# Decoder layer on one core: head 0's first projection in the gate chain, and the delta-rule loop begun at body 1

## What is computed

```python
mixed = hidden_states @ W_qkv                       # 512 -> 8*128 (q) + 8*128 (k) + 16*128 (v)
mixed = _causal_conv_silu(mixed.transpose(0, 2, 1), conv_w).transpose(0, 2, 1)   # 4 taps
z = (hidden_states @ W_z).reshape(Bb, Tt, HV, DV)
beta = sigmoid(hidden_states @ W_b)
g = -jnp.exp(A_log) * softplus(hidden_states @ W_a + dt_bias)
q = _l2norm(q) * DK ** (-0.5);  k = _l2norm(k)      # each key head serves two value heads
def step(S, inp):                                   # over 256 tokens
    S = S * exp(gt)
    v_adj = (vt - einsum('bhk,bhkv->bhv', kt, S)) * bt
    S = S + kt * v_adj
    o = einsum('bhk,bhkv->bhv', qt, S)
o = o * rsqrt(mean(o * o) + EPS) * norm_weight * silu(z)
return o.reshape(Bb, Tt, VALUE_DIM) @ W_out
```

## Time and profile before

| | us |
|---|---|
| median of three runs | 2235.8 |
| profiled execution | 2231.07 |
| its span, first to last instruction | 2229.3 |
| `prepare`, to its last instruction | 0 to 64.95 |
| clearing block and what lies around it | 64.95 to 70.61 |
| opening of the main block | 70.61 to 81.3 |
| body 0, body 1 | 81.3 to 124.9, to 166.1 |
| body 32 begins | about 1414.7 |
| mean granted clock of the span | 0.962 |

### The profile page before, as it was taken

The page is one execution under the profiler, slowest core; times in us unless marked ns, Lnnn a source line. Parts: engine busy times, 40 slices in busy tenths (PEclk is TensorE's granted clock), DMA queues, the critical chain, the costliest instruction groups (busy, mean ns, idle before and its releaser), DMA issues. The chain is left out here.

```text
span 2229.3 us, 55828 instructions
## 1 busy us (share of the span) xinstructions
PE 2042.1 (92%) x19672; PEld 1482.0 (66%) x19672; DVE 1724.6 (77%) x4017; ACT 1524.6 (68%) x4326; POOL 708.7 (32%) x610
## 2 busy tenths in 40 slices
PE   5699999999999999999999999858999999857998
PEld 3477777777777777777777777646666666534544
DVE  7677877877877877877877877645788888856997
ACT  3588888888888887887888887635656666633443
POOL 6312112112112112112112112113676777741332
PEclk8799999999999999999999999779999999978999
DMA  3100100100100100100100000053333333231111
GB/s 78 53 10 14 43 10 15 42 10 19 38 10 19 38 10 19 38 10 19 38 10 20 23 10 19 11 179 107 96 106 105 102 99 96 62 123 48 60 59 43
DMA packets 119728, 106.33 MB, mean 48 GB/s; under 512 B 11984, under 2 KB 93904, under 8 KB 119632
## 3 DMA queue, kind: packets, MB, share of 16 engines
q1 hardware_dynamic: 119632, 105.29, 15.0%
HBM read 70.66 MB, written 34.60 MB: 47 GB/s over the span
## 5 line engine op out<-in xcount | busy, mean ns | idle before, releaser
L589 PE MATMUL proj<-xn_hi,w_lo 128*128 x768 | 362.4, 472 | 0.0
L590 PE MATMUL proj<-xn_lo,w_hi 128*128 x768 | 303.8, 396 | 0.0
L591 PE MATMUL proj<-xn_hi,w_hi 128*128 x768 | 303.0, 394 | 0.0
L976 DVE SCALAR_TENSOR_TENSOR qkv<-conv_in,taps,qkv 128x512 f32<-128x512 f32 x384 | 278.2, 745 | 0.0
L1202 POOL TENSOR_TENSOR o_scale<-o_var,neg_half 128x4 f32<-128x4 f32 x68 | 67.6, 1010 | 549.1 <-DVE o_var L997 549.0
L1218 POOL TENSOR_TENSOR k_len<-sumsq,pos_half 128x4 f32<-128x4 f32 x32 | 46.9, 1466 | 571.6 <-DVE sumsq L1151 571.6
L1095 DVE TENSOR_TENSOR i_less_r<-bank_c,join_mask 128x256 f16<-128x256 f32 x330 | 124.3, 417 | 101.9 <-PE bank_c L653 101.3
L895 ACT ACTIVATE inv<-bank_b 128x256 f16<-128x256 f32 x330 | 111.3, 382 | 96.1 <-PE bank_b L674 92.5
L591 PEld LDWEIGHTS proj<-xn_hi,w_hi 128*128 128x128 f32 x768 | 144.2, 188 | 34.4
L589 PEld LDWEIGHTS proj<-xn_hi,w_lo 128*128 128x128 f32 x768 | 144.3, 188 | 24.0
L1699 ACT ACTIVATE probs_t<-ps_s 128x512 f32<-128x512 f32 x128 | 69.6, 596 | 130.4 <-PE ps_s L1547 130.3
(11 more groups left out here) (288 smaller groups left out, 5799.2 us busy)
## 6 DMA issues: line engine op xcount, KB each, us to landing
out_t<-o_out SPq DMA_DIRECT2D x68, 256.0 KB, 2.0
o_raw<-out_t SPq DMA_DIRECT2D x32, 512.0 KB, 5.4
w_raw<-in_L_attn_W_qkv_dram SPq DMA_DIRECT2D x32, 256.0 KB, 2.8
wq_dram<-wq_q SPq DMA_DIRECT2D x48, 128.0 KB, 2.0
x_sb<-in_x_dram SPq DMA_DIRECT2D x16, 256.0 KB, 2.7
w_raw<-in_L_attn_W_z_dram SPq DMA_DIRECT2D x16, 256.0 KB, 2.7
x_in<-in_x_dram SPq DMA_DIRECT2D x16, 256.0 KB, 5.6
wq_raw<-in_L_ffn_w_gate_dram SPq DMA_DIRECT2D x16, 256.0 KB, 2.7
```

The costliest lines, as they stand in the source:

```text
L589: pe.matmul(out, w_lo[:, k, cols], sh.xn_hi[:, k, tok], start=(k == 0), stop=False)
L590: pe.matmul(out, w_hi[:, k, cols], sh.xn_lo[:, k, tok], start=False, stop=False)
L591: product = pe.matmul(out, w_hi[:, k, cols], sh.xn_hi[:, k, tok], start=False, stop=(k == KT - 1))
L976: dve.scalar_tensor_tensor(out=out, in0=conv_in[:, j, :, k:k + T], scalar=taps[:, j, k:k + 1], in1=out, op0=ALU.mult, op1=ALU.add).then_in ...
```

## The change

The nine tiles that a projection uses move to `prepare`'s allocations, as `sh.*`. `prepare` makes pair 0's whole projection of head 0 with them. `delta_rule` starts at n = 1: its block `zero` gives every semaphore the count that body 0 would have left; the mask, the decay sums, the gates, the tanh of z and the key lengths for body 1 stand ahead of the loops. TensorE gets a loop of its own for pairs 1 to 3 of head 0.

```diff
@@ prepare, sync: behind the small loads
+                for j in range(TILES):
+                    load_tile(j)
@@ prepare, gpsimd: first
+                pool.memset(sh.conv_in[:, :, :, 0:TAPS - 1], 0.0).then_inc(pad_done, 1)
@@ prepare, vector
                 dve.tensor_scalar(sh.norm_half[:, :], norm_raw[:, :], 0.5, None, ALU.mult)
+                split(0)
+                split(1)
+                dve.wait_ge(taps_done, 1)
...
+                dve.tensor_copy(sh.taps[:, 0:2, :], by_kind[:, :, 0, :])
+                dve.tensor_copy(sh.taps[:, 2:4, :], sh.conv_half[:, 2 * HK:2 * HK + 2, :]).then_inc(taps_done, 1)
+                dve.wait_ge(taps_done, 2)
+                split(2)
                 dve.wait_ge(consts_done, 2)
...
                 dve.reciprocal(um1[:, :, :], um1[:, :, :]).then_inc(gate_dve, 1)
+                split(3)
...
                 dve.tensor_scalar(g[:, :, :], g[:, :, :], -1.0, -MAX_DECAY, ALU.mult, ALU.max).then_inc(gate_dve, 1)
+                split(4)
+                convolve(0)
                 dve.wait_ge(gate_dve, 13)
...
                 dve.tensor_tensor(g_lo[:, :, :], g[:, :, :], g_hi[:, :, :].bitcast(F32), ALU.subtract).then_inc(gate_dve, 1)
+                split(5)
+                convolve(1)
                 dve.wait_ge(gate_act, 7)
...
+                for j in range(2):
+                    silu(j)
+                for j in range(2, 4):
+                    convolve(j)
+                dve.wait_ge(ss_ps, 1)
+                dve.tensor_scalar(sh.sumsq[:, :], ps_t[0][:, 0:8], EPS, None, ALU.add)
@@ prepare, tensor: behind the transposes of the gates
+                def project(j):
+                    pe.wait_ge(w_lo_done, j + 1)
+                    if j < 2:
+                        pe.wait_ge(xt_done, 2 * R)
+                        pe.wait_ge(lo_done, 4 + BEFORE)
+                        pe.wait_ge(hi_done, 4)
+                    else:
+                        pe.wait_ge(proj_ev, j - 1)
...
+                for j in range(3):
+                    project(j)
                 pe.wait_ge(consts_done, 2)
                 pe.wait_ge(gate_dve, 13)
...
+                for j in range(3, TILES):
+                    project(j)
+                pe.wait_ge(sq_done, 1)
+                pe.wait_ge(proj_ev, TILES - 1)
+                for c in range(8):
+                    last = pe.matmul(ps_t[0][:, c:c + 1], ...)
+                last.then_inc(ss_ps, 1)
@@ prepare, scalar
                 for i in (R - 2, R - 1):
                     copy_gates(i, i % 2)
+                    split(i - R + 2)
+                split(2)
...
                 act.activation(ln_u[:, :, :], u[:, :, :], ACT.Ln).then_inc(gate_act, 1)
+                split(3)
+                for j in range(2):
+                    tile_copy(j)
+                    split(4 + j)
+                tile_copy(2)
                 act.wait_ge(cum_ps, 1)
...
+                tile_copy(3)
+                act.wait_ge(conv, 2 * (TAPS - 1))
+                act.activation(sh.th[:, :, :], sh.qkv[:, 0:2, :], ACT.Tanh).then_inc(th_done, 1)
+                tile_copy(4)
+                act.wait_ge(silu_done, 2)
+                act.activation(sh.th[:, :, :], sh.qkv[:, 0:2, :], ACT.Square).then_inc(sq_done, 1)
+                tile_copy(5)
@@ delta_rule, block zero
-                    sp.dma_start(w_raw[j][:, :, :], ...)
...
+            for done in once:
+                act.sem_inc(done, 1)
...
-                pool.memset(qkv[:, :, :], 0.0)
                 pool.memset(z_silu[:, :, :], 0.0)
-                pool.memset(k_len[:, :], 1.0)
                 pool.memset(pos_half[:, :], 0.5)
-                for s in S:
-                    pool.memset(o[s][:, :, :], 0.0)
-                    pool.memset(inv_r[s][:, :, :].bitcast(F32), 0.0)
+                pool.memset(o[0][:, :, :], 0.0)
+                pool.memset(inv_r[0][:, :, :].bitcast(F32), 0.0)
+                for done in twice:
+                    pool.sem_inc(done, 2)
...
-                dve.memset(conv_in[:, :, :, :], 0.0)
-                for z in (z_raw, z_th):
-                    dve.memset(z[:, :, :], 0.0)
-                dve.memset(gate[:, :, :], 0.0)
-                dve.memset(gate_off[:, :, :], 0.0)
+                dve.memset(o[1][:, :, :], 0.0)
+                dve.memset(inv_r[1][:, :, :].bitcast(F32), 0.0)
...
-                dve.memset(g_cols[:, :, :], 0.0)
@@ delta_rule, tensor
-                    decay_sums(0, s, None)
-                with pe.Fori(0, HK) as g:
+                    decay_sums(1, s, 1)
+                with pe.Fori(1, PAIRS) as p:
+                    step(p, 0, p)
+                with pe.Fori(1, HK) as g:
@@ delta_rule, scalar
-                for j in range(LATE):
-                    split(0, j)
-                mask_gates(0, None)
+                mask_gates(1, 1)
+                act.activation(z_th[:, :, :], z_raw[:, :, :], ACT.Tanh, scale=0.5).then_inc(z_th_done, 1)
                 for g in range(HK):
-                    step(PAIRS * g, True, g, None)
+                    if g:
+                        step(PAIRS * g, True, g, None)
@@ delta_rule, vector: as on scalar, and ahead of it
-                for j in range(LATE):
-                    split(j, j + 1)
-                head_taps(0)
+                dve.tensor_copy(g_cols[:, :, :], sh.gates[:, 2:4, 8:16]).then_inc(cols_done, 1)
+                key_gate(1)
+                off_gate(1)
@@ delta_rule, gpsimd
+                pool.tensor_tensor(k_len[:, :], sumsq[:, 4:8], pos_half[:, :], ALU.pow).then_inc(len_done, 1)
+                with pool.Fori(1, STEPS) as n:
+                    step(n, True)
```

More of the change, by code:

```diff
@@ L23 @@
 W_COLS = 6 * P
+RAW_TILES = 3
 TAPS = 4
@@ L75, in prepare @@
     sh.gates = keep("gates", [P, 2 * (STEPS + 1), 16], F32)
+    sh.w_raw = [keep(f"w_raw{i}", [P, KT, P], F32) for i in range(RAW_TILES)]
+    sh.w_hi = keep("w_hi", [P, KT, W_COLS], F32R)
+    sh.w_lo = keep("w_lo", [P, KT, W_COLS], F32R)
+    sh.taps = keep("taps", [P, 4, TAPS], F32)
+    sh.conv_in = keep("conv_in", [P, 4, 2, T + TAPS - 1], F32)
+    sh.qkv = keep("qkv", [P, 4, 2 * T], F32)
+    sh.th = keep("th", [P, 2, 2 * T], F32)
+    sh.z_raw = keep("z_raw", [P, 2, 2 * T], F32)
+    sh.sumsq = keep("sumsq", [P, 8], F32)
     with ExitStack() as st:
@@ L242, in high_part, with split, convolve, silu @@
                                         xn_t[:, odd, k, :].rearrange("p (k t) -> p k t", k=KT)).then_inc(hi_done, 1)
+                def split(j):
+                    dve.wait_ge(w_hi_done, j + 1)
+                    cols = slice(P * j, P * j + P)
+                    dve.tensor_tensor(sh.w_lo[:, :, cols], sh.w_raw[j % RAW_TILES][:, :, :], sh.w_hi[:, :, cols].bitcast(F32),
+                                      ALU.subtract).then_inc(w_lo_done, 1)
+                def convolve(j):
+                    moved = sh.qkv[:, j, :].rearrange("p (b t) -> p b t", b=2)
+                    dve.wait_ge(proj_ev, j + 1)
+                    dve.wait_ge(pad_done, 1)
+                    for k in range(TAPS - 1):
+                        if k:
+                            dve.wait_ge(conv, (TAPS - 1) * j + k)
+                        dve.scalar_tensor_tensor(out=moved, in0=sh.conv_in[:, j, :, k:k + T], scalar=sh.taps[:, j, k:k + 1],
+                                                 in1=moved, op0=ALU.mult, op1=ALU.add).then_inc(conv, 1)
+                def silu(j):
+                    dve.wait_ge(th_done, 1)
+                    dve.scalar_tensor_tensor(out=sh.qkv[:, j, :], in0=sh.th[:, j, :], scalar=1.0, in1=sh.qkv[:, j, :],
+                                             op0=ALU.add, op1=ALU.mult).then_inc(silu_done, 1)
                 dve.memset(sh.gates[:, 0:2, :], 0.0)
@@ L340, in _ @@
                 last.then_inc(ba_turned, 1)
+                def project(j):
[6 more added lines that the diff above has]
+                        pe.wait_ge(proj_ev, j - 1)
+                    cols = slice(P * j, P * j + P)
+                    for k in range(KT):
+                        pe.matmul(ps_t[j % 2][:, :], sh.w_lo[:, k, cols], sh.xn_hi[:, k, 0:N2], start=(k == 0), stop=False)
+                        pe.matmul(ps_t[j % 2][:, :], sh.w_hi[:, k, cols], sh.xn_lo[:, k, 0:N2], start=False, stop=False)
+                        last = pe.matmul(ps_t[j % 2][:, :], sh.w_hi[:, k, cols], sh.xn_hi[:, k, 0:N2], start=False,
+                                         stop=(k == KT - 1))
+                    last.then_inc(proj_ps, 1)
+                for j in range(3):
+                    project(j)
                 pe.wait_ge(consts_done, 2)
@@ L499, in _ @@
             def _(pe):
-                pe.sem_inc(ss_ps, FIRST)
+                for done in (w_hi_done, w_lo_done, proj_ps, proj_ev):
+                    pe.sem_inc(done, TILES)
+                for s in S:
+                    for done in (r_ps, r_done, x_ps, x_done, t_done):
+                        pe.sem_inc(done[s], LEVELS)
```

(10 more changed lines are left out.)

98 lines of the change are left out of this document (57 added, 41 removed).

## The result

| | before | after |
|---|---|---|
| median of the runs timed together, us | 2236.67 (4 runs) | 2201.76 (4 runs, 2201.1 to 2202.54) |
| ratio, 95% interval | | 0.9847 [0.9835, 0.9859] |
| profiled execution, us | 2231.07 | 2202.18 |
| its span, us, and mean clock | 2229.3, 0.962 | 2200.5, 0.962 |
| first stage ends | 64.95 | 78.41 |

The account below looks back on a forecast made before the run. It took TensorE's filled delta-rule loop as the bound, with stretches ahead nearly empty of TensorE work and VectorE ending the gate chain. +13.4 - 1.7 - 4.6 - 41.7 = -34.6 us, from the 2235.8 median to 2201; range 2194 to 2210.

Parts of the forecast that it names:

- point 1: Main loop: one body goes and a new first body of 43.1 us replaces two taking 84.8; gain 41.7 us.
- point 2: Loop's opening: masks start after one small copy, other work hides behind them; 6.1 us instead of 10.69, gain 4.6.
- point 3: Clearing block: fewer clears but new semaphore increments at 48 ns; body from 4.6 to 2.9 us, gain 1.7.
- One sign of being wrong: Clearing block: the prediction called itself wrong if this block came out above 4.7 us.
- point 4: Gate chain: VectorE's 14.0 us of added work, less covered waits, plus collisions with GpSimd, lengthens it by 13.3 us.
- Rival C: Gate chain: GpSimd's block masks also collide with VectorE's low parts and tap copies, +3.0 us, 2204; chance 0.10.
- point 5: Gate chain on TensorE: tiles 3 to 5 start cold, squares end at 78.2, together with VectorE; +13.4 us.
- the last signature in the prediction: Gate chain's end: if TensorE's sums of squares stand clearly ahead of VectorE's last tap, VectorE alone sets the end.
- A: Clearing block and gate chain: semaphores nearly free, collisions fall into waits; -38.7 us, 2197; chance 0.15.
- B: Gate chain: TensorE stays at 1.2 GHz for all six tiles, +24 instead of +13.4, 2212; chance 0.10.
- D: Gate chain: tiles go in lockstep for raw buffers, 61 us later, so slower than before, 2249; chance 0.03.
- E: Main loop: TensorE's new loop copy makes its queue late at two first bodies, 2 to 4 us, 2205; chance 0.06.

Follow-up runs that it names:

- experiment 2: The changed kernel run again with no edit: 2200.52 us (4 runs), ratio 0.9837 to the kernel before.
- experiment 8: Changed kernel plus fourteen 512-column TensorE products that nothing reads, in the clearing block and around the decay sums: 2196.02 us.
- experiment 4: Changed kernel without GpSimd's block masks (clear and 14 selects) and without its join-mask products: 2196.24 us.
- experiment 3: Changed kernel with GpSimd's four join-mask products replaced by a clear of the same tile: 2198.12 us.
- experiment 5: Changed kernel with the clearing block's semaphore increments dealt out evenly by number to all five engines: 2204.76 us.
- experiment 6: Changed kernel with the clearing block's increments dealt out by each engine's measured price, 12 on TensorE and 26 on ScalarE: 2197.94 us.
- experiment 7: Changed kernel with the taps of the v tiles and the sums of squares moved from the first stage into the main block's opening: 2197.99 us.
- experiment 9: Changed kernel with all of pair 0's projection work placed behind the gate table instead of woven into the gate chain: 2216.85 us.
- the second pair: Profiled executions of the kernel before and the changed kernel, both run again with no edit; medians 2236.44 and 2200.52 us.

## Why the prediction was right, step by step

The forecast was the likeliest case, 2201, and the medians are 2201.76 and 2200.52. That it met them within 1 us is in part luck, as the last paragraph of this section shows: two steps were off and the traces up to the end of the loop show a smaller gain than the medians. Of its parts:

**One body goes** (point 1): 43.6 + 41.2 - 43.7 = 41.1 us against 41.7. The size hangs on when the clock comes back, which experiments 2 and 8 show to be worth up to 2.7 us. Not forecast: bodies 2 to 31 take 0.8 to 1.0 us more in both pairs of traces. Single bodies differ by 0.2 to 0.4 us, and in the later kernels by other bodies. The traces show where most of it sits: ahead of the scores' products TensorE pauses six times for its own issue, 1.0 us in all (five times, 0.9 us, in the second trace); in the kernel before no such pause shows in bodies 2 to 31, and 0.3 us in two in its second trace. Why the issue is late stays open; that it is the place of the code is argued, not shown.

**The opening** (point 2): 6.17 us against 6.1. The tanh, the gates and the key lengths hid as said.

**The clearing block** (point 3) is the step that failed in size: 5.09 us against 3.96, a gain of 0.57 instead of 1.7. The mechanism, ScalarE's 59 increments as the last to end, was right (its last start is 83.2), the price wasn't. I took a register instruction's length on TensorE's queue, 48 ns, for an increment on ScalarE's; it costs 0.069 us between two starts, and 0.15 on TensorE. The bound from the earlier trace rows, 0.08 with the barrier, was nearer. One sign of being wrong, a clearing block above 4.7 us, needs reading: 4.7 was the upper end of the block's body in point 3, and the body took 4.1 us (79.2 to 83.3), while the stretch with its barriers took 5.09. A learner should name the stretch that such a bound is for.

**The gate chain** (point 4): +13.46 us against +13.3, but not for the reasons given. The forecast's own end without the join collisions and without the mask collisions was 78.25 - 3.0 = 75.25; experiment 4 shows 73.64. On that come 2.33 us for the block masks, where I had put no cost, and 2.44 us for the join products, where I had put 3.0. The sum is 78.41. The term for the added work was right: by the starts in experiment 4 it is 15.3 us (six low parts 4.7 with their wait for `xn_lo`, twelve taps 8.9, silus 1.2, copies and sums 0.5), against 14.0 + 1.1. What failed is the treatment of collisions. For the block masks I had put a gain of 0.3 us on the two casts. They cost 2.33, of which 1.4 stood in the old 64.95 already (experiment 4), so the term is +0.9. For the join products I had put 3.0 - 1.4 = 1.6; with the measured 2.44 it is 1.0. Some 0.6 us of short gaps between operations that had waited for each other went as well, which I hadn't counted. These errors of 0.6 to 1.2 us nearly cancel: that +13.3 was met to 0.2 us is luck.

Rival C's mechanism is true, though of the operations that it names only one copy of the taps was slow (1.00 us); low parts 2 and 3 took their usual 0.69 and 0.63, and most of the rest of the loss was in the casts and `um`. I had read one row, `ln_u` at 0.49 us, as proof that selects don't block VectorE, while another row of the same group, `ones_r` at 0.94 us for 128x128 elements, showed a collision with GpSimd's mask building (0.22 us alone). With only its own 3.0 us on top of my sum, C would have given 2204. What the prediction quotes of the Trainium skill (SBUF — State Buffer, Who interferes with whom) is on instructions with two SBUF inputs, and I had weighed it down; experiments 3 and 4 agree with it in `g` (1.01 us, 0.42 without join products) and `um` (0.75 us, 0.43 without selects). The copy and the casts have one input, so that sentence doesn't cover the larger part of the mask loss. The traces also show that not every pair meets: `ln_u` at 60.03 took 0.42 us amid the selects. The low part of tile 0 beside `xn_lo` cost the 1.1 us forecast (two low parts took 2.39 us, 1.27 by the price of the earlier trace rows).

**TensorE as a check** (point 5): wrong in its middle, harmless in the end. Tile 2 fell to half clock and tiles 3 to 5 didn't, so the last tile ended at 72.9 instead of 76.3. In experiments 5 and 6, whose first stage is the same code, tile 2 ran at full clock (mean 1.00 from 58.65 to 63.10), and the stage still ended at 78.47 and 78.37. "Both engines end together" is refuted: VectorE alone set the end, as the last signature in the prediction allowed. Experiments 3 and 4 say the same: with GpSimd's work away VectorE's time fell, and the end with it. In experiment 7 more than 4.5 us of VectorE's work moved away, and the stage ended 3.3 us earlier, because ScalarE's square then ended it.

**The rivals.** A is refuted in both parts, increments and collisions. B: the clock fell, for one tile, not for six. D: the loads ran ahead, and nothing went in lockstep; experiment 9, with the weaving undone, shows what order is worth, 9.8 us, and even that stays 20 us faster than before. E: no body after the second is 2 us longer; the 1.0 us over 30 bodies, in pauses for issue of at most 0.2 us, is all there is. Its price, 1.2 us from the earlier trace rows, was no row of the loops either: that pause lies in body 32, and up to 1414 us TensorE's only wait of that kind took 0.2 us.

**The sum.** The measured terms give 13.46 - 0.57 - 4.52 - 41.1 = -32.7 us, and with the 1.0 of the later bodies body 32 begins 31.7 us earlier (32.8 in the second pair). Against the profiled time the forecast was 2196.5, and the profiled execution came out at 2202.18. Of this difference of 5.7 us the terms explain 1.9, the later bodies 1.0, and 2.9 lie behind the loop. The medians differ by 34.9 and 35.9 us, 2 to 4 more than the loop shows, and it is this difference that brings the forecast's 34.6 so near. By the intervals of the ratios the gain is 31.5 to 36.9 us in the first comparison, which holds its traces' 31.7, and 32.9 to 40.3 in the second, which just misses its traces' 32.8. Whether the last 2 to 4 us are chance behind the loop or something real there stays open; no trace shows an instruction that the change made faster there.

## What to carry to other kernels

When work is moved into a chain that looks half idle, add up busy time and the pauses that take it, and then every pair of engines that will now run side by side: a three-line list of the GpSimd instructions with the VectorE instructions above them would have shown both collisions here. Look at the same time for what the old chain already loses to them, since that part is no cost of the change. Price a queue instruction by the distance between starts on its own engine, not by its duration or by another engine's, and deal many of them out by those prices. A sum that comes out right proves its total only; take the terms out one by one before a term is used again.

## What was new about the hardware

- A standalone semaphore increment costs 0.069 us on ScalarE's queue, 0.06 on SyncE's, 0.09 on VectorE's and 0.15 on TensorE's, while the profile gives it 17, 17, 21 and 51 ns. They run beside the engine's unfinished work: in experiment 8 TensorE's fillers ran from 79.1 to 82.0 us and its 20 increments from 79.2 to 82.1, and the clearing block ended no later than without the fillers.
- A copy of 8 elements a partition took 1.00 us beside a GpSimd clear and 0.16 us without it (experiment 4). The cast of `ones_r` went from 0.22 to 1.17 us, a two-operand product of 256 columns from 0.43 to 0.75, and others of that size, amid the same selects, lost nothing.
- How long a kernel stays at half clock after a pause differs between executions: the changed kernel's first body took 43.7 and 42.0 us. With filling products it took 41.0 and 41.1 in the two kernels that had the clock back ahead of it.
- The stages behind the loop, unchanged in every kernel, took between 814.6 and 823.5 us in the profiled executions: more than most of the steps measured here, which is why single steps were read from stage ends and not from total times.
